# Sparse experts planned twice: the last four sequences routed between the first expert tiles

## The reference, cut to what matters

```python
x = x + ga * attention(layernorm(x) * (1 + ca) + sa)       # 16 sequences
h = layernorm(x) * (1 + cb) + sb
t = h * rsqrt(mean(h * h) + 1e-5) * norm_scale
logits = t @ gate_w + gate_b                               # 8 experts
top_v, top_i = top_k(logits, 2); probs = softmax(top_v)
for each expert e:                                         # only its own tokens in the kernel
    u = t @ w1[e] + b1[e]                                  # 128 -> 512
    g, l = min(u[::2], 7), clip(u[1::2], -7, 7)
    y = (g * sigmoid(1.702 * g) * (l + 1)) @ w2[e] + b2[e] # 256 -> 128
    acc += prob of e * y
x = x + gb * (h + acc)
```

## Time and profile before

| | |
|---|---|
| median of 3 runs | 1067.23 us (1066.64 to 1077.73) |
| span of the profiled execution | 1003.5 us |
| attention loop with the rounds behind it | about 345 to 716 us |
| plan, padding, last scatters | 716 to 739 us |
| expert tiles | 739 to 963 us |
| read-back, sum and output | 964 to 1003.5 us |
| busy over the span: PE, DVE, ACT, POOL | 83%, 82%, 62%, 56% |

### The profile page before, as it was taken

The page is one execution under the profiler, slowest core; times in us unless marked ns, Lnnn a source line. Parts: engine busy times, 40 slices in busy tenths (PEclk is TensorE's granted clock), DMA queues, the critical chain, the costliest instruction groups (busy, mean ns, idle before and its releaser), DMA issues.

```text
span 1003.5 us, 22806 instructions
## 1 busy us (share of the span) xinstructions
PE 837.3 (83%) x7439; PEld 645.8 (64%) x7439; DVE 827.6 (82%) x2204; ACT 619.4 (62%) x1669; POOL 563.5 (56%) x573
## 2 busy tenths in 40 slices
PE   6887972899999579999999999994149999999900
PEld 6854652444454268888888888883038888889800
DVE  3987769899997586789999999997638888888848
ACT  3475128899983474587787767746236666666600
POOL 1221018568760534336888888887727676767720
PEclk9999895799999879999999999996569999999955
DMA  5230541333233050000111111111243333233168
GB/s 153 82 90 1 143 134 46 130 105 138 90 127 127 9 145 19 2 10 26 37 44 34 37 36 45 36 37 47 95 122 94 89 90 89 89 95 97 54 227 296
DMA packets 74479, 84.47 MB, mean 84 GB/s; under 512 B 14254, under 2 KB 64361, under 8 KB 72188
## 3 DMA queue, kind: packets, MB, share of 16 engines
q1 hardware_dynamic: 56492, 60.06, 19.7%
q0 software_dynamic: 8704, 18.11, 5.4%
q10 hardware_dynamic: 9168, 4.87, 1.6%
HBM read 59.33 MB, written 23.67 MB: 83 GB/s over the span
## 4 chain that ended last, share of the span: by engine, by line
PE 51%; DVE 6%; DMA 2%; issue 2%; POOL 1%; SPq 1%; ACT 1%; POOLq 0%; DVEq 0%; ACTq 0%
PE ps L2432 13%; PE ps L2194 11%; PE ps L2451 6%; PE ps L2210 3%; PE ps L2272 2%; PE ps L2185 2%; PE ps L2417 2%; PE ps L2331 2%; PE ps L2311 2%; PE ps L2205 1%; POOL rows_of L1479 1%; PE ps L2156 1%; PE ps L2171 1%; PE ps L2259 1%; DVE x_tok L2128 1%
## 5 line engine op out<-in xcount | busy, mean ns | idle before, releaser
L1470 POOL TENSOR_TENSOR kvb<-qk,v 128x1024 f32<-128x1024 f32 x64 | 126.7, 1984 | 74.7 <-DVE qk L1854 50.4
L1479 POOL DMA_INDIRECT rows_of<-payb,posu x128 | 144.1, 1126 | 40.6 <-issue 27.0
L1115 PE MATMUL ps<-masked,ew 128*128 128x512 f32 x256 | 129.9, 623 | 4.2 <-DVE masked L1043 3.5
L2194 PE MATMUL ps<-con,kvb 128*128 128x128 f32 x1024 | 126.0, 276 | 0.0
L2194 PEld LDWEIGHTS ps<-con,kvb 128*128 128x128 f32 x1024 | 119.4, 192 | 1.0 <-issue 1.0
L1504 POOL DMA_INDIRECT parts<-h,dest x72 | 72.8, 1011 | 55.0 <-ACT h L1756 33.3
L1043 DVE TENSOR_TENSOR masked<-f_t,wide 128x512 f32<-128x512 f32 x128 | 88.6, 710 | 9.7 <-PE ps L1115 9.4
L1830 DVE TENSOR_TENSOR qc<-ps,qk 128x1024 f32<-128x1024 f32 x64 | 78.0, 1219 | 17.9 <-PE ps L2194 17.3
L1747 ACT ACTIVATE nrm<-qk 128x512 f32<-128x512 f32 x72 | 45.4, 630 | 72.8 <-DVE qk L2104 72.7
L1504 POOL DMA_INDIRECT parts<-gx,dest x72 | 74.9, 1040 | 25.6 <-issue 23.3
L2451 PE MATMUL ps<-w,f_t 128*128 x576 | 76.1, 275 | 0.0
(11 more groups left out here) (354 smaller groups left out, 2237.7 us busy)
## 6 DMA issues: line engine op xcount, KB each, us to landing
wide<-hot_dram SPq DMA_DIRECT2D x16, 1024.0 KB, 4.6
kvb<-rows_of SPq DMA_DIRECT2D x72, 132.0 KB, 2.1
toep<-taps_dram SPq DMA_DIRECT2D x16, 512.0 KB, 6.1
x_tok<-in_x_dram SPq DMA_DIRECT2D x16, 256.0 KB, 3.1
out_dram<-x_tok ACTq DMA_DIRECT2D x16, 256.0 KB, 5.6
rows<-rows_dram SPq DMA_DIRECT2D x16, 192.0 KB, 3.2
kvb<-parts SPq DMA_DIRECT2D x6, 512.0 KB, 6.9
rows<-rows_dram SPq DMA_DIRECT2D x16, 128.0 KB, 4.5
```

The costliest lines, as they stand in the source:

```text
L1115: nc.tensor.matmul(ps[:, w % 2, :], ew0[:, e, :], masked[e % 4][:, :], start=False, stop=(e == E - 1)).then_inc(s["product"], 1)
L1470: nc.gpsimd.tensor_tensor(kv[g % KB][:, :, :].rearrange("p e (h d) -> p e h d", h=H), k_in, v_in, ALU.mult).then_inc(s["kv"], 1)
L1479: nc.gpsimd.indirect_dma_start(rows_of, bass.IndirectOffsetOnAxis(ap=posu[w % 2][:, slot, t:t + 1], axis=0), pay[w % PB][:, t, :], None).t ...
L2194: last = nc.tensor.matmul(cum(g)[:, e, :], kv[g % KB][:, e, :], k("upto"), start=True, stop=True)
```

## The change

1. The plan is made twice. Once AW = 10 sequences are counted (`ranks` now also gives the totals after sequence 9), DVE plans the first FT = 32 tiles in its step 16, between the last pieces of attention. The assertion says that 10 sequences always fill that many whole tiles. The other 40 tiles are planned within tiles 18, 19 and 20 (PLAN = 18).
2. The loops are cut: PE stops after step 17, DVE after 16, ACT after 19, POOL after 16. What is left of sequences 12 to 15 runs between the first 20 tiles: four rounds of ROUND = 5 tiles, in each engine's `drain(v)`.
3. PE's pieces stand in front of a tile's first-layer products, behind the turning of the next tile. `residual(15)` and `moments(15)` come in DVE's tiles 0 and 1. `gated` and `added` of the last four come in tiles 22 to 29.
4. The two roots of the late norms go from ACT (log, exp) to POOL (pow). The late softmax of two uses Tanh, so ACT keeps one table.
5. ACT's copy of the first-layer weights is gone. SP loads them from device memory for each tile, 256 KB into one of WC = 4 buffers. The norm scale goes into ACT's copy of x. `glu` moves from DVE to ACT (two Relu activations).
6. PE's banks: one for x, one for y, where there were two of each. There are YW = 16 buffers for finished tiles. POOL scatters a finished tile's rows in every second tile from tile 3 on, and without a break behind tile 19.
7. Padding is written at tile 28, and SP waits for the last scatters before it loads tile 32. `Tiles` and `passes` become plain loops.

```diff
+        AW = 10
+        FT = 32
+        YW = 16
+        assert 2 * C * P * AW - E * (SP - 1) > (FT - 1) * SP
 # SP
+                    for w in range(max(0, AW - PB), AW):
+                        sp.wait_ge(s_scat[w % PB], 16 * SCATTERS * (w // PB + 1))
                     sp.wait_ge(s["place"], 1)
+                    for v in range(BT):
+                        if v == FT - PADS:
+                            pads()
+                        if v == FT:
+                            second_part()
...
+                        done(sp, "x_ps", v - V)
+                        grouped(sp, "dest", v - V)
+                        sp.dma_start(xt[:, v % V, :, :], rows_of[bass.ds(at, SP), :]...)
+                        e = expert_of(sp, packed, v)
+                        done(sp, "h_ps", v - WC)
+                        sp.dma_start(w1c[v % WC], a["w1"][:, bass.ds(e, 1), :]...)
 # POOL
-                    for n in range(B + 6):
+                    for n in range(B + 1):
...
+                    for v in range(ROUNDS * ROUND):
+                        r, at = divmod(v, ROUND)
+                        if at == 0:
+                            variance_root(B - 2 + r)
+                        if at == 1:
+                            square_root(B - 3 + r)
+                        if at == 4:
+                            for i in range(SCATTERS if r == ROUNDS - 1 else SCATTERS // 2):
+                                send(B - 4 + r, i)
+                        if at == 0 and r:
+                            for i in range(SCATTERS // 2, SCATTERS):
+                                send(B - 5 + r, i)
+                        if v >= 3 and v % 2:
+                            place_rows(placed_rows)
+                            placed_rows += 1
+                    for v in range(placed_rows, BT):
+                        place_rows(v)
 # ACT
-                    for n in range(B + 8):
+                    for n in range(B + 4):
...
+                    def drain(v):
+                        if at == 0:
+                            if r:
+                                logits_kept(B - 4 + r)
+                            squares(B - 3 + r)
+                        if at == 2:
+                            normed(B - 2 + r)
+                            weigh_late(B - 4 + r)
+                            payload(B - 3 + r)
+                        if at == 4:
+                            turned_pay(B - 3 + r)
...
+                        turned(v + 1)
+                            done(act, "hg_ps", v)
+                            # two Relu into glu, then the gelu into gs
+                        drain(v)
+                        if v >= 2:
+                            # grouped dest, rows_out(v - 2 - YW), y_ps: then yw(v - 2)
 # DVE
+                    def drain(v):
+                        if v == 0:
+                            residual(B - 1)
+                        if v == 1:
+                            moments(B - 1)
+                        if r < ROUNDS and at == 1:
+                            shifted(B - 2 + r)
+                            logits(B - 4 + r)
+                            largest(B - 4 + r)
+                            chosen(B - 4 + r)
+                        if r < ROUNDS and at == 3:
+                            placed(B - 4 + r)
+                            modulated(B - 2 + r)
+                        if v == PLAN:
+                            tiles_of_experts(True)
+                        if v == PLAN + 1:
+                            experts_of_tiles(True)
+                        if v == PLAN + 2:
+                            rows_of_tiles(True)
...
+                    for v in range(BT):
+                        # lin(v)
+                        if v < ROUNDS * ROUND and v % ROUND == 3:
+                            ranked(B - 4 + v // ROUND)
+                        product(v)
+                        if v % GT == 0:
+                            weights_and_places(v)
+                        drain(v)
 # PE
-                    for n in range(B + 6):
+                    for n in range(B + 2):
...
+                    def drain(v):
+                        if v == 0:
+                            back(B - 1)
+                        if at == 0 and r:
+                            logits(B - 4 + r)
+                        if at == 1:
+                            logits_back(B - 4 + r)
+                        if at == 2:
+                            ranks(B - 4 + r)
+                        if at == 4:
+                            turn_pay(B - 3 + r)
+                    turn(0)
+                    for v in range(BT + 2):
+                        turn(v + 1)
+                        drain(v)
+                        # first-layer products of v, then the second layer of v - 2 (waits a(v - 2), yw(v - 3))
```

More of the change, by code:

```diff
@@ new lines, in _ @@
+                    need(dve, "place", 1)
+                    ahead = pack_of(dve, 0)
+                    for v in range(BT):
+                        if v % V == 0:
+                            packed = ahead
+                        e = expert_of(dve, packed, v)
+                        bank = H_PS + 2 * (v % 2)
+                        done(dve, "h_ps", v)
+                        done(dve, "a", v - 2)
+                        for f in range(2):
+                            last = nc.vector.tensor_scalar(lin[v % 2][:, f, :], ps[:, bank + 1, f * SP:(f + 1) * SP],
+                                                           b1[:, bass.ds(e * NF + 2 + f, 1)], 8.0, ALU.add, ALU.min)
+                        last.then_inc(m["lin"], 1)
+                        if v % V == V - 2 and v + 2 < BT:
+                            dve.wait_ge(s["place"], 3 if v + 2 >= FT else 1)
+                            ahead = pack_of(dve, v + 2)
+                        if v < ROUNDS * ROUND and v % ROUND == 3:
[4 more added lines that the diff above has]
+                        drain(v)
```

589 lines of the change are left out of this document (312 added, 277 removed).

## The result

The changed kernel takes 1100.34 us (median of 4 runs, 1096.30 to 1105.77) against 1070.50 of the kernel before (4 runs): ratio 1.028, 95% interval 1.022 to 1.035. It is slower, by 30 us, and lies outside the predicted range of 1050 to 1084.

What follows compares the result with a forecast made beforehand. PE bounds the tile stage before the change, POOL's scatters the end after it: `posu` of sequence 15 at 784 us, plus 181.6 to POOL's end, 40.7 to the span's end and 63.7 outside it gave 1070 us, range 1050 to 1084.

Steps and rivals of the forecast that it cites:

- first tile's products: Start of tile 0's first-layer products on PE: at 695 us, 46 us earlier than in the profile read.
- from there to `posu` of sequence 15: Tiles 0 to 18 with the routing rounds between them: 89 us, so `posu` at 784 us; a round 22 us.
- from there to POOL's last DMA done: POOL behind `posu` of sequence 15: 136 indirect DMAs back to back at 1.33 us, 181.6 us with hand-over, ending at 965.6.
- cover of 12 us: Behind tile 18 PE finishes ahead of POOL, so up to 12 us lost by PE there costs nothing.
- Wait A: `ranks`, before first-layer products of tiles 2, 7, 12, 17, waits for DVE's choice: 3.5 us each round.
- Wait B: PE's second layer waits for `yw` to free the one y bank: 2.0 us in each of the first two rounds.
- The clock: PE's clock drops in each wait A; 3.6 us at half speed lose 1.8 us, all but 0.8 swallowed by wait B.
- rival 3: POOL's indirect DMAs grow longer, 1.43 us each in all: 136 cost 13.6 us more, 1083 us; chance 0.12.
- rival 1: POOL is the tail and its end hardly moves: 1070 us, own range 1059 to 1079; chance 0.48.
- 2 (POOL never pauses, faster): Routing pieces come on time and POOL never pauses from `posu(12)` on: 1055 us, or 1043 with shorter DMAs; chance 0.27.
- 4: PE's clock stays low through the rounds, 20 to 27 us in all: 1090 to 1097 us; chance 0.09.
- 5 (a late start): Tile 0 waits for something held for hidden; each us late is lost, counting from 8 us on; chance 0.04.

Runs made afterwards that it cites:

- e17: Kernel before, but ACT issues two plain DMAs per finished tile to fixed places instead of POOL's indirect DMAs (wrong tokens summed): 1027.96 us, ratio 0.962.
- execution shown: The profiled execution of the unchanged kernel that the prediction read: span 1003.5 us, while the median was 1067.23 us.
- before usual: A later profiled execution of the unchanged kernel, of the usual kind; in 73 such executions the span is 1058.5 to 1074.9 us.
- after: The kernel with the whole change, against the kernel before: 1100.34 us, ratio 1.028.
- e7: Changed kernel with PE's routing pieces behind a tile's first-layer products, not in front of them: 1084.27 us, ratio 1.014 to the kernel before.
- e14: Changed kernel, but ACT issues two plain DMAs per finished tile to fixed places instead of POOL's indirect DMAs (wrong tokens summed): 1030.82 us, ratio 0.966.
- e3: Changed kernel loading first-layer weights only for tiles 0 to 3 and reusing them for later tiles (output wrong): 1089.04 us, ratio 1.018 to the kernel before.
- e4: Changed kernel with first-layer weights resident and copied by ACT for each tile, as before the change: 1094.41 us, ratio 1.023 to the kernel before.
- e16: Kernel of e8 with first-layer weights resident and copied by ACT instead of loaded per tile: 1055.43 us, ratio 0.989 to the kernel before.
- e15: Kernel of e8, but ACT issues two plain DMAs per finished tile to fixed places instead of POOL's indirect DMAs (wrong tokens summed): 1024.77 us, ratio 0.962.
- e13: Kernel of e8, but POOL waits for tile 51's yw, then places tiles 42 to 51 in one train: 1083.23 us, ratio 1.015.
- e8: Changed kernel with all pieces for the last four sequences before the first tile, none between tiles: 1066.21 us, ratio 0.998 to the kernel before.
- e6: Changed kernel with a POOL multiplication behind each late send and each indirect DMA placing rows of tiles 0 to 19: 1126.95 us, ratio 1.054.
- e10: Kernel before, with POOL waiting for glu of the tile three on between a tile's two indirect DMAs: 1069.52 us, ratio 1.000.
- e5: Changed kernel with POOL placing one finished tile's rows every tile, not every second, in the first twenty tiles: 1087.97 us, ratio 1.0175.

## Why the prediction was wrong, point by point

In the sum's own terms, against the profiled execution (1105.77 us by its run):

| term | forecast | measured | off by |
|---|---|---|---|
| first tile's products | 695 | 707.7 | +12.7 |
| from there to `posu` of sequence 15 | 89 | 119.9 | +30.9 |
| from there to POOL's last DMA done | 181.6 | 235.7 | +54.1 |
| from there to the end of the span | 40.7 | 40.7 | 0 |
| outside the span | 63.7 | 1.8 | -61.9 |

The step that failed is the third: that POOL works back to back behind `posu` and so ends last, with PE ahead under a cover of 12 us. The second is under-sized. The last is wrong as well, and it hid the third: without it the miss would have been 98 us. Of the third's 54 us, the last 47 tiles at 3.64 and not 2.95 us make 32 and the gap at tile 22 makes 31, less the 12 us of cover.

**The baseline.** "The 63.7 us between span and median" were no constant outside the span. The usual execution has them inside. Of the 66 us by which its span is longer, 39 go when finished tiles leave by plain DMAs (e17). The 23 us up to the first tile do not: e17 has its first tile at 761.5, still with POOL's 128 sends. DVE waits for its own results beside the sends in both (4.6 us once), which points at the sends, but no run took them away. My sum describes an execution of the kind shown; whether the changed kernel would have met it in such an execution is open, as none of its four runs was one.

**The start.** The first plan was out at 688.75, 6 us behind the forecast 683, and SP's loads were hidden. But DVE's `g_t` started at 701.99, where the sum had it at 689.7:

```profile
693.16 0.43 PE L2337 MATMUL ps<-qc,low_heads 128*32 128x128 f32 x8
699.41 0.96 POOL L1487 DMA_INDIRECT rows_of<-payb,posu  x1 [0.30 <-issue]
701.99 0.69 DVE L1882 TENSOR_TENSOR g_t<-ps,rb 128x512 f32<-128x512 f32 x1 [6.78 <-remote]
```

PE's attention was done at 693.6, and DVE saw it 8.4 us later, 1.6 us behind POOL's eight sends (690.3 to 700.4). The tiles started at 707.7, not 695. Nearly all of this is the baseline again and not the change. The output projection behind `g_t` starts at 685.09 in the execution shown, but in before usual and in after:

```profile
700.85 2.08 PE L2272 MATMUL ps<-g_t,wo 128*128 128x512 f32 x2 [7.10 <-DVE g_t L1821]
```

```profile
702.74 2.08 PE L2399 MATMUL ps<-g_t,wo 128*128 128x512 f32 x2 [8.71 <-DVE g_t L1882]
```

So the first plan put it back by 1.9 us against the usual execution, and not by 4.6, at the lower end of my own bounds of 2 to 6.7 us.

**The rounds.** Forecast 22 us each and `posu` of sequence 15 at 784; measured 31.0, 26.5 and 35.3 us from one `posu` to the next, and 827.6. Wait A is there, at the four places named, and under-sized: 22.5 us in all (3.5 each forecast, 5.6 measured). Moving the pieces behind the products gave some 15 us (e7). Without POOL's DMAs for tiles the rounds take 25.8, 25.6 and 29.8 us (e14). Of the 43.6 us by which `posu` missed, 12.7 are the late start; of the other 30.9 (119.9 us from the first tile to it, 89 forecast), e14 with 108.1 us leaves 19.1 to sums that were short (POOL's sends still in them) and gives 11.8 to the rows of finished tiles. Wait B came as forecast, 2.0 us in each of the first two rounds, in tiles 3 and 8:

```profile
732.00 0.28 PE L2585 MATMUL ps<-b2x,one 128*128 x1 [1.85 <-ACT xg L1818]
761.94 0.28 PE L2585 MATMUL ps<-b2x,one 128*128 x1 [1.54 <-ACT xg L1818]
```

The clock was under-sized: I had about 5 us for all four rounds, and the estimate above is up to 17 more than in before usual. It follows the gaps; what it costs alone was not measured.

**POOL as the bound.** Forecast: 136 DMAs of 1.33 us back to back behind `posu` to 965.6, and PE done ahead. Measured, over the whole span:

```profile
L1528 POOL DMA_INDIRECT parts<-xg,dest x144 | 140.5, 975 | 122.1 <-ACT xg L1818 88.4
```

POOL was not the bound: it waited 88 us for ACT's `yw`, and PE set the pace to the end. The prediction had named this sign: if POOL waits for finished tiles at the end, PE was the bound. The DMAs were shorter than I took (0.975 + 0.30 us), so rival 3 is out, and so is the tail by POOL (rival 1's mechanism). The 40.7 us from POOL's last DMA to the end were right (1063.3 to 1104.0). What was mis-seen is the kind of cost that POOL's DMAs have: not their own length, but the results of PE that come late beside them. The Trainium skill (Perfetto Trace Analysis, "DMA Instruction — SWDGE (GPSIMD)") says that such a row ends with the writing of descriptors and not with the movement of data; the trace agrees: the row of the last DMA before the pause ends at 866.6, and the packets of its queue go on to 867.5. The results held back came at 871.2, 3.7 us behind the last packet.

**The tile pace and the cover.** I costed at nothing whatever PE loses behind tile 18, under 12 us of cover. There was none, and tile 22 alone lost 31 us. The 2.95 us of the earlier trace rows is the pace without disturbance; beside POOL's scatters before usual and after run at 3.6, and only the execution shown kept 2.95 beside them. The streamed weights, costed at nothing, cost 0.2 us a tile (e3, e4, e16), 11 us, but only beside the scatters: in e14 and e15 they stream, and all but two or three of the tiles 24 to 71 take 2.95.

**Rivals.** 2 (POOL never pauses, faster) fell with the rounds' length. 4 gave 1090 to 1097 for a low clock; its price is nearest and its mechanism is there in part: 90.7 of the 171.0 us of tiles 0 to 24 were at the lower clock, worth up to 17 us by the estimate, as a follower of the waits. 5 (a late start) came by 12.7 us, for a reason that it did not name: nearly all of it was in the usual execution of before already. The case that held, results that arrive late beside POOL's DMAs, was not among them. The profile I read shows none; the only sign of it was that the runs were 64 us longer than its span.

## What stays open

By the updates at 871.2 the signals were held back and not PE's work; what holds them is not shown. Nor is it shown why one execution of the kernel before was free of it, with the same DMAs: they are not enough by themselves. It is open, too, which of the three differences between indirect and plain DMAs counts, and what the sends alone cost, up to the first tile above all. Where DMAs lie sparse (two a tile) the price is about 0.3 us for each (39 to 41 us over 144); in e13's train of 24 it is 17 us over e8 plus what the quiet before it had saved (10 tiles at 2.95 and not 3.63 us, 7 us), so 1.0 us each. Whether length or density makes the difference e6 and e10 do not settle.

## What to carry to other kernels

Compare a profile's span with its run's time before any sum is made; if tens of us are missing, the profile may be of an unusual execution, and the missing time may belong to a stage that the change lengthens. Profile the old kernel once more first. An engine off the critical path can cost by how it issues: here a queue of POOL's indirect DMAs that was let go at once went with hand-overs of PE up to 31 us late. Such work is better let out as it comes (e5), or put where PE waits for nobody. And before routing or other chains of small steps are put between tiles, run them alone first: here a round took 11.5 us alone and 26 to 35 between tiles, more than the idle time that it was to fill.

## What the hardware showed unexpectedly

A result of PE was seen up to 31 us late, by ACT, DVE and SP at one moment, while POOL issued indirect DMAs 1.26 us apart; with POOL quiet the same tiles ran at 2.95 us without a late result (e13). The signals of ACT and DVE in the same stretch of after were at most 0.13 us late, but in before usual DVE waited 4.6 us for its own. The bytes moved do not do it: 203 GB/s of plain DMAs left PE busy 50.00 of 50 us (e14). And one execution of the kernel before ran its 144 indirect DMAs beside the tiles without any of this. SP's DMA issue of 1.39 us at 855.71, where most take 0.33, does not belong to it: e14 has one of 1.68 us at 854.3 with no indirect DMA near.
